# A ternary quantizer's odd tiles computed by ScalarE's Sign passes and two VectorE passes, in an eight-core attention and feed-forward layer

## What is computed

```python
def _absmean_core(W):
    gamma = jnp.mean(jnp.abs(W)) + EPS
    Ws = W / gamma
    Wq = jnp.sign(Ws) * jnp.minimum(jnp.round(jnp.abs(Ws)), 1.0)
    return (Wq, gamma)
...
h = jnp.einsum('btd,hd->bth', x, absmean(W_fc))      # W_fc: 4096 x 1024
h = jax.nn.gelu(h, approximate=False)
h = layernorm(h, ln_w, ln_b)
return jnp.einsum('bth,dh->btd', h, absmean(W_proj)) # W_proj: 1024 x 4096
...
x = x + attn(layernorm(x)); x = x + ffn(layernorm(x))
```

## Time and profile before

| what | us |
|---|---|
| time, median of 2 runs | 3664.11 (3663.99 to 3664.23) |
| the profiled execution's own time | 3667.61 |
| its span on the slowest core, core 6 | 3666.1 |
| spans of the other cores | 3651.8 to 3662.7 |
| quantizing loop over W_fc on core 6, first pass to end of the last | 464.17 to 577.14 |
| first matmul of the main loop | 639.81 |

### The profile page before, as it was taken

The page is one execution under the profiler, slowest core; times in us unless marked ns, Lnnn a source line. Parts: engine busy times, 40 slices in busy tenths (PEclk is TensorE's granted clock), DMA queues, the critical chain, the costliest instruction groups (busy, mean ns, idle before and its releaser), DMA issues.

```text
span 3666.1 us, 66863 instructions; the slowest of 8 cores (3651.8 to 3666.1 us)
## 1 busy us (share of the span) xinstructions
PE 2900.5 (79%) x22170; PEld 1960.5 (53%) x22170; DVE 2239.1 (61%) x5462; ACT 868.4 (24%) x2133; POOL 71.7 (2%) x148
## 2 busy tenths in 40 slices
PE   0002242998989898989898989898989898989896
PEld 0002140665666565656565656565656565656564
DVE  5667775656565656565656666666656565656544
ACT  1114301222222222222222222222222222222211
POOL 0000202000000000000000000000000000000000
PEclk9999999999999999999999999999999999999998
DMA  4438542000000000000000000000000000000000
GB/s 146 125 123 258 188 134 64 7 7 18 7 13 13 13 13 13 13 13 13 13 13 13 13 12 13 13 13 13 13 12 13 13 8 17 7 19 1 12 1 12
DMA packets 38403, 130.26 MB, mean 36 GB/s; under 512 B 7216, under 2 KB 7344, under 8 KB 38064
## 3 DMA queue, kind: packets, MB, share of 16 engines
q1 hardware_dynamic: 18864, 67.22, 6.0%
q10 hardware_dynamic: 9216, 33.56, 2.9%
q0 software_dynamic: 9984, 25.20, 1.9%
HBM read 109.15 MB, written 16.78 MB: 34 GB/s over the span
## 4 chain that ended last, share of the span: by engine, by line
PE 72%; DVE 12%; DMA 5%; ACT 4%; DVEq 3%; issue 3%; ACTq 1%; POOL 1%; SPq 0%; POOLq 0%
PE proj_ps L229 36%; PE fc_ps L685 34%; DVEq L50 3%; DVE cols L51 3%; DVE x1s L51 3%; DMA x1s<-wpT 3%; DMA xs<-wfcT 2%; DVE bnp L51 1%; PE trp_ps L666 1%; ACT ATT L51 1%; DVE gps_t L51 1%; DVE rrq L51 1%; ACT qf_t L51 1%; ACT qp_t L51 1%; ACTq L50 1%
## 5 line engine op out<-in xcount | busy, mean ns | idle before, releaser
L229 PE MATMUL proj_ps<-qp_t,gps_t 128*128 128x512 bf16 x6144 | 1435.3, 384 | 171.4 <-DVE gps_t L51 171.2
L685 PE MATMUL fc_ps<-l2t_t,qf_t 128*128 128x256 bf16 x12288 | 1446.9, 275 | 0.7 <-ACT l2t_t L51 0.7
L685 PEld LDWEIGHTS fc_ps<-l2t_t,qf_t 128*128 128x128 bf16 x12288 | 1200.6, 99 | 181.0 <-issue 2.1
L229 PEld LDWEIGHTS proj_ps<-qp_t,gps_t 128*128 128x128 bf16 x6144 | 604.6, 99 | 813.1 <-issue 212.5
L51 ACT ACTIVATE g<-fc_ps 128x256 f32<-128x256 f32 x512 | 196.3, 383 | 2032.8 <-PE fc_ps L685 1883.2
L51 DVE TENSOR_TENSOR S<-S,g 128x256 f32<-128x256 f32 x496 | 211.0, 425 | 761.7 <-ACT g L51 758.5
L51 DVE SCALAR_TENSOR_TENSOR rrq<-g,lnw_c,gps_t 128x256 f32<-128x256 f32 x512 | 248.3, 485 | 38.8 <-issue 0.6
L51 ACT ACTIVATE l2t_t<-trp_ps 128x128 bf16<-128x128 f32 x768 | 212.8, 277 | 133.6 <-PE trp_ps L666 73.6
L51 DVE TENSOR_TENSOR gps_t<-rrq,gps_t 128x256 bf16<-128x256 f32 x512 | 217.6, 425 | 40.9 <-issue 3.7
L51 DVE TENSOR_TENSOR S<-S,gsq 128x256 f32<-128x256 f32 x496 | 211.1, 426 | 42.5 <-issue 6.4
L51 ACT ACTIVATE gsq<-g 128x256 f32<-128x256 f32 x512 | 213.3, 417 | 43.0 <-issue 1.8
(11 more groups left out here) (127 smaller groups left out, 1375.4 us busy)
## 6 DMA issues: line engine op xcount, KB each, us to landing
x1s<-wpT ACTq DMA_DIRECT2D x64, 512.0 KB, 4.1
xs<-x SPq DMA_DIRECT2D x64, 512.0 KB, 3.5
xs<-wfcT SPq DMA_DIRECT2D x64, 512.0 KB, 4.6
out<-x1s POOLq DMA_DIRECT2D x32, 512.0 KB, 2.9
x1s<-wvT POOLq DMA_DIRECT2D x8, 512.0 KB, 7.8
x1s<-woT POOLq DMA_DIRECT2D x8, 512.0 KB, 7.1
l2t_t<-gps_t POOLq DMA_DIRECT2D x96, 0.2 KB, 1.5
xs<-ident SPq DMA_DIRECT2D x1, 64.0 KB, 9.0
```

Of the source, the lines that this page charges most:

```text
L229: last = tensor.matmul(out=proj_ps[tg][:, 512 * hh:512 * hh + 512], lhsT=gps[jj % 2][s][:, 128 * tg:128 * tg + 128], rhs=qp[jj][:, 512 * h ...
L685: last = tensor.matmul(out=fc_ps[j % 2][:], lhsT=qf[d][:, 128 * j:128 * j + 128], rhs=l2t[i % 2][s][d][:], start=(s == 0 and d == 0), stop ...
```

## The change

The tiles with an odd number are no longer quantized by three passes on VectorE. ScalarE computes two Sign activations for each (16 tiles, 32 activations), the one with the bias -0.5 as bf16 straight into the tile's place in `qf_t`, the one with +0.5 as f32 over the loaded weights in `xs[1]`. It raises `B_sgf`, a semaphore that was declared and unused. VectorE waits for it in the tile's turn, adds the two (a bf16 and an f32 operand, bf16 result), and multiplies the bf16 result by 0.5 in place. The tiles with an even number are as they were. The order of tiles on VectorE, the two buffers, the transfers and what they wait for (`B_q`) are unchanged. ScalarE's loop stands between its two groups of small copies.

```diff
@@ scalar
                     scalar.inc(ss_abT, 1)
+                for k in range(1, 32, 2):
+                    scalar.wait_ge(B_x2s[k % 2], 16 * (k // 2 + 1))
+                    if k == 1:
+                        scalar.wait_ge(B_g3, 2)
+                    dstf = qf[k // 4][:, 1024 * (k % 4):1024 * (k % 4) + 1024]
+                    scalar.activation(out=dstf, in_=xs[k % 2][:], func=AF.Sign,
+                                      scale=rcg[0][:], bias=mhalf[:])
+                    scalar.activation(out=xs[k % 2][:], in_=xs[k % 2][:], func=AF.Sign,
+                                      scale=rcg[0][:], bias=phalf[:])
+                    scalar.inc(B_sgf, 1)
                 for s in range(3):
                     scalar.wait_ge(st_abT, 4 + s)
@@ vector
             for t in range(32):
-                vector.wait_ge(B_x2s[t % 2], 16 * (t // 2 + 1))
-                if t == 0:
-                    vector.wait_ge(B_g3, 2)
-                vector.tensor_scalar(out=U[:], in0=xs[t % 2][:], scalar1=rcg[0][:],
-                                     scalar2=0.5, op0=OP.mult, op1=OP.is_gt)
-                vector.tensor_scalar(out=V[:], in0=xs[t % 2][:], scalar1=rcg[0][:],
-                                     scalar2=-0.5, op0=OP.mult, op1=OP.is_lt)
                 dst = qf[t // 4][:, 1024 * (t % 4):1024 * (t % 4) + 1024]
-                vector.tensor_tensor(out=dst, in0=U[:], in1=V[:], op=OP.subtract)
+                if t % 2 == 0:
+                    vector.wait_ge(B_x2s[t % 2], 16 * (t // 2 + 1))
+                    if t == 0:
+                        vector.wait_ge(B_g3, 2)
+                    vector.tensor_scalar(out=U[:], in0=xs[t % 2][:], scalar1=rcg[0][:],
+                                         scalar2=0.5, op0=OP.mult, op1=OP.is_gt)
+                    vector.tensor_scalar(out=V[:], in0=xs[t % 2][:], scalar1=rcg[0][:],
+                                         scalar2=-0.5, op0=OP.mult, op1=OP.is_lt)
+                    vector.tensor_tensor(out=dst, in0=U[:], in1=V[:], op=OP.subtract)
+                else:
+                    vector.wait_ge(B_sgf, (t + 1) // 2)
+                    vector.tensor_tensor(out=dst, in0=dst, in1=xs[t % 2][:], op=OP.add)
+                    vector.tensor_scalar_mul(out=dst, in0=dst, scalar1=0.5)
                 vector.inc(B_q, 1)
             vector.wait_ge(st_uv, 1)
```

## The result

| | kernel before | changed kernel |
|---|---|---|
| time, median | 3663.98 us (8 runs) | 3687.19 us (9 runs) |
| ratio to before | 1 | 1.0063, 95% interval 1.0052 to 1.0074 |
| the profiled execution's own time | 3667.61 | 3687.01 |
| its slowest core's span | 3666.1 (core 6) | 3685.1 (core 7) |
| loop over W_fc on that core | 464.17 to 577.14, 112.97 us | 463.42 to 596.09, 132.67 us |

The change costs 23.2 us, 0.6% of the time, where 21.8 was forecast. In some executions of several kernels four cores, in one also the other four, had a lower granted clock and took longer; ratios and medians here leave them out.

What follows compares the result with a forecast made beforehand. The W_fc loop was taken as bound by a ring of transfer and passes, not VectorE; odd turns growing from 7.14 to 8.67 us lengthen the loop by 21.8 us, 3664.11 + 21.8 = 3685.9 us, range 3676 to 3697.

Steps and rivals of the forecast that it cites:

- The bound: W_fc loop: each buffer's transfer and passes run in series, 7.14 us a turn; VectorE needs only 5.96 of it.
- The prices: Odd tile's added work: sum 1.23 us, bf16 scaling 0.42, two Sign passes 2.55, hand over to VectorE 0.14.
- The turn: Odd buffer in the W_fc loop: 4.25 + 2.55 + 0.14 + 1.73 = 8.67 us instead of 7.14.
- the rival with the shortest landings: W_fc transfers land in 3.53 us, turn 8.21, total +14.9 us or 3679.0; chance 0.14.
- The even tiles: Even buffer in the W_fc loop: needs only 7.14 us a turn, so it gets ahead and waits for the odd one.
- any such wait as a sign of being wrong: W_fc loop: VectorE still waiting for transfers before `U` would refute the forecast, which expected no such idle time.
- VectorE's wait before the sum: Odd tiles of the W_fc loop: VectorE idle some 3.9 us a turn, released by ScalarE.
- Behind the loop: After the W_fc loop: the shift goes through whole, with 62 to 63 us to the first matmul as before.
- a main loop of the same length: Main loop after the W_fc stage: length unchanged, with nothing put on TensorE's 22 us more idle time before it.
- If the main loop moves by itself: Main loop: any change of its own was named as a sign that the forecast is wrong.
- Bandwidth as the bound: W_fc loop: memory bandwidth sets the turn, so time stays at 3664.1 us or falls below; chance 0.05, shared with another case.
- The dearer scaling and Sign passes: Odd tiles: scaling at 0.75 us, +27.1 total, 3691.2, chance 0.10; Sign passes doubled, 3724, chance 0.03.

Runs made afterwards that it cites:

- the pass in the ring: Changed kernel with ScalarE's first Sign pass of each odd tile issued twice before B_sgf is raised: 3710.01 us, ratio 1.0118.
- outside it: Changed kernel with a third Sign pass per odd tile, behind the raising of B_sgf on a tile nobody waits for: 3691.42 us, ratio 1.0069.
- the pair on one chip: Changed kernel and kernel before, both unaltered, profiled again on the same chip: ratios 1.0062 and 1.0005.
- six buffers: Changed kernel with six W_fc buffers, bf16 second Sign and comparisons, odd buffers released by ScalarE: 3625.40 us, ratio 0.9890.
- the issue 0.5 us earlier: Changed kernel with the odd buffer released after VectorE's sum, before the scaling: 3683.46 us, ratio 1.0049.
- four and bf16: Changed kernel with four W_fc buffers, bf16 second Sign and comparisons, odd buffers released by ScalarE: 3627.78 us, ratio 0.9903.

## Why the prediction was right, point by point

*The bound.* Right. The ring of transfer and passes bound the loop, not VectorE and not bandwidth: the pass in the ring cost 21.2 us and outside it 0.4, and four buffers took 16.4 us off the kernel before without any other edit (112.4 to 96.0).

*The prices.* The scaling without a row, put at 425 ns by ratio from the earlier trace rows, took 427. The sum took 1225 ns as its twin in the earlier trace rows, the Sign passes 1240 as in the earlier trace rows, the hand over 0.15 us for 0.14. Tile 1 ended 4.71 us after the loop's start (468.14 - 463.43), as computed. (The 3.99 us for a landing is the mean of all cores; the fifteen of core 6 have 4.01, which changes nothing.)

*The turn.* 8.67 forecast, 8.53 measured. The mis-sized term is the transfer with issue and release: 4.25 us, taken over from the kernel before with its hesitations. The landings on the chain of core 7 had a mean of 3.90 us, and over all cores 3.83 where the kernel before had 3.99. That is a third of the way to the rival with the shortest landings (3.53): 15 x 0.14 = 2.1 us, which makes +19.7 of +21.8 on the profiled cores.

*The even tiles.* Right from the second turn on; `U` waited once more for its transfer, 2.05 us at tile 2, when the even ring had no lead yet. The prediction had named any such wait as a sign of being wrong; one in sixteen does not touch the sum, because the odd ring sets the turn. VectorE's wait before the sum was 55.0 / 15 = 3.7 us a turn, forecast 3.9.

*Behind the loop.* The 62.6 us to the main loop were unchanged, and TensorE's longer idle time cost nothing there. The step that failed is the last one, "a main loop of the same length". It was 2.8 us longer, 3.4 in the pair on one chip, a term that the prediction put at nothing because the change doesn't touch the main loop's code. "If the main loop moves by itself" was one of its own signs of being wrong. What it left out is that the change takes 32 instructions out of VectorE's stream and puts 81 into ScalarE's. The miss is in the opposite direction of the landings', 2.1 us, and so the sum came closer to the measured 23.2 than its parts: part of the agreement is luck. The remaining microsecond has no term; the start of the loop alone varies more between the cores (454 to 464 us).

*The rivals.* Bandwidth as the bound is refuted by four buffers and 200 GB/s. The dearer scaling and Sign passes did not come. Shorter landings came by a third, and alone they would have given some 3683.8.

## What to carry to other kernels

An idle engine doesn't make moved work free: where a buffer is loaded again only after its passes, every pass on it lies in series with the transfer, whichever engine runs it, and the turn is transfer plus all passes plus each hand over. Add these up for the ring that gets the new pass before counting what the relieved engine saves. If the relieved engine's idle time is already ended by the transfer, give the ring depth first; with four buffers the same edit gained 17 us instead of costing 19.

## What the runs showed of the hardware that was not expected

- A landing is not a constant. The same 512 KB took 3.83 us in the mean with the changed kernel, 3.99 before, 4.5 for the odd tiles where ScalarE released them (3.8 to 4.1 for the even ones beside them), 4.7 to 4.9 at 200 GB/s and 6.0 to 6.8 (medians, core 6) with six buffers. With the issue 0.5 us earlier it was 3.80 on one core and 4.24 on its neighbour.
- TensorE's small product beside the loop stretched as more data moved. Its matmuls stood still without any wait for 5.9 us in the kernel before (mean of the cores, 3.4 to 8.5) and 6.8 in the changed kernel, but for 15.2 with four buffers, 16.1 with four and bf16, and 20.6 with six (136 and 121 GB/s on the slowest core from 463 us on, then 200, 222 and 236). The traces show what ended these holes. All that are longer than 0.1 us, 73 in the kernel before and 87 with six buffers, stand at places of TensorE's stream that are multiples of 128 matmuls (with their 128 weight loads) apart. Each of those above 0.3 us, 50 and 80, ended 1.2 to 1.6 us after a transfer of 16 KB of the kind "instruction" on queue 8 had ended. Such a transfer ran from 489.57 to 490.48 us on core 6 of the kernel with six buffers, and the longest hole there ended at 491.90:

```profile
PE fc_ps L645 <- issue: 25.8, 11, 4.3
...
491.90 0.19 PE L645 MATMUL fc_ps<-lnbb,qp_t 128*128 128x1 bf16 x1 [4.26 <-issue]
```

By these times a stream of short instructions waits for its own code, and it waited longer in the kernels that moved more data beside it. No run moved the code's transfers by themselves.

- 32 waits that do nothing, put far ahead of the main loop, moved it by 1.7 us, and the holes of 0.4 us stand 128 instructions apart in VectorE's stream. Differences of 0.1% between kernels can come from there.
